# Exponentials of two pairs at once, rotating sum slots, and norms moved to GpSimd in a fused transformer, expert and state-space kernel

## The reference

```python
h = layernorm(x) * (1 + ca) + sa
x = x + ga * attention_block(h)       # linear attention with decay, then a silu layer
h = layernorm(x) * (1 + cb) + sb      # experts: 8 of 128 -> 512 -> 128
x = x + gb * sum_e weight_e * (gelu(h @ w1[e] + b1[e]) @ w2[e] + b2[e])   # top 2 of 8
h = layernorm(x) * ...                # state space, 256 channels, 16 states n
dA = exp(dt * A[:, n])                # 128 x 512 per channel half, state and chunk
H  = dA * H + (dt * xc) * B[n]        # a scan over the tokens
y  = sum_n H * C[n]; y = y * silu(z); x = x + ga * (y @ W_out)
h = layernorm(x) * ...                # real part of an inverse FFT of a weighted FFT
x = x + gb * (h @ w_fft + bias)
```

## Time and profile before

| | us |
|---|---|
| median of 3 runs (605.8 to 610.0) | 607.29 |
| the profiled execution | 606.43 |
| its span in the trace | 604.4 |
| TensorE busy | 482.4 (80%) |
| VectorE busy | 428.9 (71%) |
| ScalarE busy | 363.4 (60%) |
| GpSimd busy | 313.2 (52%) |

### The profile page before, as it was taken

How to read it: one execution, slowest core, us unless ns; L and a number is a source line. 1 busy time by engine, 2 the same in 40 slices (tenths; PEclk the granted TensorE clock), 3 DMA queues, 4 the chain that set the end, 5 groups by cost and what they waited for, 6 DMA issues and landing times.

```text
span 604.4 us, 6869 instructions
## 1 busy us (share of the span) xinstructions
PE 482.4 (80%) x2346; PEld 337.7 (56%) x2346; DVE 428.9 (71%) x723; ACT 363.4 (60%) x507; POOL 313.2 (52%) x220
## 2 busy tenths in 40 slices
PE   3869876769899999979869988789897497667573
PEld 3457544434588886757756677657586443233222
DVE  4766798964534334058997779997879985997961
ACT  0531442224664676689999999799988656634201
POOL 3224976866111011314686649767557946566541
PEclk9986999989999999999999989999989779897797
DMA  8700000000000000401866553765725703111000
GB/s 294 272 1 0 1 1 1 2 0 0 1 0 2 2 1 0 142 1 35 193 147 139 151 139 87 180 136 144 168 75 148 165 20 104 70 63 42 17 0 17
DMA packets 15010, 44.74 MB, mean 74 GB/s; under 512 B 2241, under 2 KB 7745, under 8 KB 12545
## 3 DMA queue, kind: packets, MB, share of 16 engines
q0 software_dynamic: 2448, 17.83, 14.5%
q1 hardware_dynamic: 11952, 25.57, 12.4%
q10 hardware_dynamic: 576, 0.92, 0.5%
HBM read 25.31 MB, written 1.18 MB: 44 GB/s over the span
## 4 chain that ended last, share of the span: by engine, by line
PE 24%; ACT 13%; DVE 12%; issue 6%; POOL 3%; DMA 3%; POOLq 0%; ACTq 0%; DVEq 0%
DVE Hs L761 6%; PE pO L1231 5%; DVE pCT L748 4%; ACT dA L985 3%; PE pY L1274 3%; PE pY L1317 3%; ACT gel L973 3%; PE pH L1219 2%; ACT L985 2%; ACT L973 2%; PE pH L1221 2%; PE pH L1220 2%; ACT ln_x L835 2%; PE pH L1274 2%; DMA Acc<-ZS 1%
## 5 line engine op out<-in xcount | busy, mean ns | idle before, releaser
L1231 PEld LDWEIGHTS pO<-w_e,gel 128*128 128x128 f32 x1024 | 124.8, 195 | 14.2 <-issue 8.8
L1231 PE MATMUL pO<-w_e,gel 128*128 128x128 f32 x1024 | 127.2, 279 | 1.4 <-DVE X L732 1.1
L761 DVE TENSOR_TENSOR_SCAN Hs<-dA,HL,pCT 128x512 f32<-128x512 f32 x96 | 117.7, 1268 | 8.1 <-POOL Zev L382 3.8
L382 POOL TENSOR_TENSOR ZS<-Hs,Crow 128x1024 f32<-128x1024 f32 x32 | 76.5, 2392 | 58.3 <-DVE Hs L761 58.3
L973 ACT ACTIVATE gel<-pH,b_e 128x512 f32<-128x512 f32 x128 | 85.9, 687 | 33.3 <-PE pH L1221 32.6
L985 ACT ACTIVATE dA<-dt,a_neg 128x512 f32<-128x512 f32 x128 | 81.9, 710 | 21.0 <-DVE Hs L761 20.7
L748 DVE TENSOR_TENSOR pCT<-u,pB 128x1024 f32<-128x1024 f32 x64 | 78.3, 1224 | 16.7 <-PE pB L1299 15.5
L1219 PE MATMUL pH<-h2h,w_e1h 128*128 128x512 f32 x128 | 57.8, 452 | 22.6 <-ACT gel L973 21.4
L382 POOL TENSOR_TENSOR Zev<-Hs,Crow 128x1024 f32<-128x1024 f32 x26 | 62.8, 2420 | 16.0 <-DVE Hs L761 15.2
L732 DVE SCALAR_TENSOR_TENSOR X<-pO,wts,X 128x128 f32<-128x128 f32 x128 | 35.9, 343 | 43.2 <-PE pO L1231 43.1
L438 POOL TENSOR_TENSOR ZA<-Qsb,S 128x1024 f32<-128x1024 f32 x16 | 38.0, 2374 | 33.6 <-DVE S L656 32.0
(11 more groups left out here) (225 smaller groups left out, 878.1 us busy)
## 6 DMA issues: line engine op xcount, KB each, us to landing
Crow<-c_rows SPq DMA_DIRECT2D x32, 512.0 KB, 4.0
Acc<-ZS POOLq DMA_DIRECT2D x10, 1024.0 KB, 8.5
Acc<-Zev POOLq DMA_DIRECT2D x7, 1024.0 KB, 7.7
w_e<-in_w_e SPq DMA_DIRECT2D x2, 2048.0 KB, 10.4
X<-in_x SPq DMA_DIRECT2D x4, 256.0 KB, 7.0
out<-h2T SPq DMA_DIRECT2D x4, 256.0 KB, 2.2
S<-in_w_mod ACTq DMA_DIRECT2D x2, 384.0 KB, 4.7
w_cx<-in_conv_row SPq DMA_DIRECT2D x1, 512.0 KB, 9.7
```

The source lines that it names most:

```text
L382: pool.tensor_tensor(Z, Hs[:, 2 * o:2 * o + 2, 0:w], Crow[:, 2 * (p % NCB) + o:2 * (p % NCB) + o + 1, 0:w].to_broadcast([P, ND, w]), ALU.m ...
L761: vec.tensor_tensor_scan(Hs[:, 2 * o + d, 0:w], dA[:, 4 * (p % 2) + 2 * o + d, 0:w], pU[:, d, 0:w], HL[:, d, n:n + 1] if c else 0.0, ALU.m ...
L1231: ins = mm(pO[:, j * P:(j + 1) * P], gel[:, n % NG, j * P:(j + 1) * P], w_e2[:, NK * (g % E) + k, :], start=(k == 0 and j == 0), stop=(k = ...
```

## The change

- `decays`: three groups of slots in dA; in odd pairs ScalarE makes the exponentials of pairs p+1 and p+2 in one go, in even pairs none.
- `pair`: up 0 and up 1 of expert g+1 are issued in pair p, between down 1 and the stages "B"; row_b of the next pair's first state moves ahead of down 1.
- The norm (`ln_apply`) goes from ScalarE to four GpSimd operations in `ln`; the two small ones that made its bias go. The cast of BCf to ST goes to GpSimd too.
- `ln_turn` of the next chunk moves from C of k = 4 to a new place "U" in k = 5: on TensorE after the first row_b and before up 2, on ScalarE between the second and third gelu.
- Zev, ZS and the two Acc become three rotating slots `Zt`: the sum of a chunk lies where the even pairs of the chunk before lay.

```diff
@@ later_stages
-                             (2, "end", "ln_stats", tail), (3, "apply", "ln_apply", tail), (3, "C", "ln_turn", tail, 2),
+                             (2, "end", "ln_stats", tail), (3, "C", "ln_turn", tail, 2),
-                    plan += [(4, "mid", "ln_stats", front), (4, "apply", "ln_apply", front), (4, "C", "ln_turn", front, 1),
+                    plan += [(4, "mid", "ln_stats", front), (5, "U", "ln_turn", front, 1),
...
@@ sums
+        def acc_of(c):
+            return Zt[:, 2 * (c % 2), :, 0:WIDTHS[c]]
+        def z_of(p):
+            c, k = divmod(p, NP)
+            if k == 0 and not alone(p):
+                return acc_of(c)
+            return Zt[:, 1 if k % 2 else 2 - 2 * (min(c, ALONE // NP) % 2), :, 0:WIDTHS[c]]
...
@@ gpsimd ln
-                pool.wait_ge(s["ln_xn"], L[0])
-                pool.tensor_scalar(ln_nm[:, 0:J], ln_mv[:, 0:J, 0], -1.0, None, ALU.mult)
                 link(pool.tensor_scalar(ln_ve[:, 0:J], ln_mv[:, 0:J, 1], EPS, None, ALU.add))
                 link(pool.tensor_tensor(ln_rs[:, 0:J], ln_ve[:, 0:J], mhalf[:, 0:J], ALU.pow))
-                pool.tensor_tensor(ln_nb[:, 0:J], ln_nm[:, 0:J], ln_rs[:, 0:J], ALU.mult).then_inc(s["ln_rstd"], 1)
+                pool.wait_ge(s["ln_tr"], L[0])
+                for j in range(J):
+                    ins = pool.tensor_scalar(ln_x[:, j, :], rows_of(X, c)[:, j, :], ln_mv[:, j, 0:1], ln_rs[:, j:j + 1],
+                                             ALU.subtract, ALU.mult)
+                ins.then_inc(s["ln_xn"], 1)
...
@@ gpsimd output
+                Z = z_of(p)[:, part, :]
                 if p >= ALONE + 2:
                     pool.wait_ge(s["mam_y"], totals(p - 2))
-                elif k == 0 and not alone(p):
-                    Z = Acc[:, c % 2, part, 0:w]
-                    if c >= 2:
-                        pool.wait_ge(s["mam_y2"], 2 * (c - 1))
...
+                elif p >= 2 and o == 0 and sums(p - 2):
+                    pool.wait_ge(mam_s[p % 2], 16 * sums(p - 2))
+                if k == 2 and c and p < ALONE + 2 and o == 0:
+                    pool.wait_ge(s["mam_y2"], 2 * c)
...
@@ gpsimd rows
+                link(pool.tensor_copy(st, bc))
...
@@ scalar decays
-                if p >= 2:
-                    act.wait_ge(s["mam_sc"], 4 * (p - 1))
+                if p >= 3:
+                    act.wait_ge(s["mam_sc"], 4 * (p - 2))
...
@@ scalar, the list
                 if 0 <= p + AHEAD < NL * E:
-                    hidden(p + AHEAD, range(NK))
-                if 0 <= p + 1 < NL * NP:
-                    decays(p + 1)
+                    hidden(p + AHEAD, (0, 1))
+                run(p, stages, "U")
+                if 0 <= p + AHEAD < NL * E:
+                    hidden(p + AHEAD, (2, 3))
+                for q in (p + 1, p + 2) if p % 2 else ():
+                    if 0 <= q < NL * NP:
+                        decays(q)
                 run(p, stages, "AB")
-                run(p, stages, ("apply",))
                 run(p, stages, "C")
...
@@ tensor pair
-                if moe:
-                    up(g, 0)
-                    up(g, 1)
+                if any(at == "U" for at, *_ in stages) and not moe:
+                    run(p, stages, "U")
                 if 0 <= p < NL * NP:
                     row_b(2 * p + 1)
+                if moe:
+                    run(p, stages, "U")
                 if moe:
                     up(g, 2)
                     up(g, 3)
...
                 if moe:
                     down(g, 0)
-                    down(g, 1)
                 if not early and 0 <= 2 * p + 2 < NL * NS:
                     row_b(2 * p + 2)
+                if moe:
+                    down(g, 1)
+                if g + 1 < NL * E:
+                    up(g + 1, 0)
+                    up(g + 1, 1)
                 run(p, stages, "B")
```

More of the change, by code:

```diff
@@ L157, in build @@
         rank = sb("rank", [P, NJ, E])
-        dA = sb("dA", [P, 2 * 2 * ND, TC])
+        dA = sb("dA", [P, 3 * 2 * ND, TC])
         Hs = sb("Hs", [P, 2 * ND, TC])
-        Zev = sb("Zev", [P, 2 * ND, TC])
-        ZS = sb("ZS", [P, 2 * ND, TC])
+        Zt = sb("Zt", [P, 3, 2 * ND, TC])
         Crow = sb("Crow", [P, 2 * NCB, TC])
@@ L210, in stage_bank @@
         def stage_bank(p, at):
-            return (2 if p < ALONE else 0) + int(at == "B")
+            return (2 if p < ALONE else 0) + int(at in ("B", "U"))
         def tail_bank(c):
@@ L283, in later_stages @@
             for stage in (("A", "total", NL * NP - 1), ("end", "gate", last), ("A", "project", last), ("end", "tail_x", last),
-                          ("end", "bias", last), ("mid", "ln_stats", last), ("apply", "ln_apply", last),
+                          ("end", "bias", last), ("mid", "ln_stats", last),
                           ("A", "ln_turn", last, 2), ("A", "fft", last)):
@@ L473, in rows @@
                 st, bc = ST[:, c % 2, 0:w], BCf[:, c % 2, 0:w]
-                pool.wait_ge(s["mam_st0"], c + 1)
-                pool.wait_ge(s["ln_rstd"], L[0])
+                pool.wait_ge(s["mam_bcs"], c + 1)
+                pool.wait_ge(s["ln_xn"], L[0])
                 for name, count in done.items():
@@ L497, in gate @@
                 for d in range(ND):
-                    pool.tensor_tensor(y2[:, d, 0:w], Acc[:, c % 2, d, 0:w], half_of(gz, c)[:, d, :],
+                    pool.tensor_tensor(y2[:, d, 0:w], acc_of(c)[:, d, :], half_of(gz, c)[:, d, :],
                                        ALU.mult).then_inc(s["mam_y2"], 1)
@@ L534, in ln_stats @@
                 Xc = rows_of(X, c)
-                vec.wait_ge(s["ln_rstd"], L[0])
+                vec.wait_ge(s["ln_xn"], L[0])
                 L[0] += 1
@@ L828, in _ @@
             nc.scalar.activation(silu_c[:, :], cols[:, COL["c0"]:COL["c0"] + 2], ACT.Silu).then_inc(s["silu_c_ready"], 1)
-            def ln_apply(c):
-                act.wait_ge(s["ln_rstd"], A[0] + 1)
-                act.wait_ge(s["ln_tr"], A[0])
-                for j in range(blocks(c)):
-                    ins = nc.scalar.activation(ln_x[:, j, :], rows_of(X, c)[:, j, :], ACT.Identity,
-                                               bias=ln_nb[:, j:j + 1], scale=ln_rs[:, j:j + 1])
-                ins.then_inc(s["ln_xn"], 1)
-                A[0] += 1
             def ln(dest, c, m, b, high=None):
@@ L950, in rows @@
                 nc.scalar.copy(BCf[:, c % 2, 0:w], PS[b][0:96, 0:w]).then_inc(s["mam_bcs"], 1)
-                act.wait_ge(s["mam_bcs"], c + 1)
-                nc.scalar.copy(ST[:, c % 2, 0:w], BCf[:, c % 2, 0:w]).then_inc(s["mam_st0"], 1)
             def dt_part(c, d, b):
@@ L996, in run @@
                         continue
-                    if stage == "ln_apply":
-                        ln_apply(c)
-                    elif stage in ("ln_turn", "route", "turn", "x_part", "rows", "dt_part", "z_part"):
+                    if stage in ("ln_turn", "route", "turn", "x_part", "rows", "dt_part", "z_part"):
                         {"ln_turn": turned, "route": route, "turn": turn, "x_part": x_part, "rows": rows, "dt_part": dt_part,
@@ L1312, in total @@
                 first = k == 0 or p == ALONE
-                Z = [Zev, ZS][p % 2]
+                Z = z_of(p)
                 for o in range(2):
@@ L1316, in total @@
                     for d in range(ND):
-                        ins = mm(pY[d][:, 0:w], ident[:, :], Z[:, 2 * o + d, 0:w], start=(first and o == 0),
+                        ins = mm(pY[d][:, 0:w], ident[:, :], Z[:, 2 * o + d, :], start=(first and o == 0),
                                  stop=(k == NP - 1 and o == 1))
@@ L1323, in total @@
                         for o in range(2):
-                            ins = mm(pY[d][:, 0:w], ident[:, :], Acc[:, c % 2, 2 * o + d, 0:w], start=False, stop=False)
+                            ins = mm(pY[d][:, 0:w], ident[:, :], acc_of(c)[:, 2 * o + d, :], start=False, stop=False)
                 ins.then_inc(s["mam_y"], 1)
```

22 lines of the change are left out of this document (6 added, 16 removed).

## The result

The changed kernel takes 651.65 us (median of 4 runs, 650.55 to 654.38) against 606.84 of the kernel before beside it: ratio 1.0748, 95% interval 1.071 to 1.0786. It is slower by 44.8 us, where 19.6 was forecast: the direction was right, the size was not, and 652 lies above the range of 603 to 638. The profiled execution took 650.55, its span 648.5.

The account below looks back on a forecast made before the run. It took a loop between TensorE and ScalarE, not one full engine, to bound the kernel. Mixed part +7.8, experts alone +4.2, norms and cast -1.8, clock +9.4 make +19.6: 626.0 for that execution, median 627; range 603 to 638 us.

Parts of the forecast that it names:

- The loop: Mixed part, odd pairs: eight exponentials stand before the next gelu, so up 2 to next up 2 takes 10.9 us.
- The other signs: Granted clock 0.50 three or more times a chunk; ScalarE some 10 us less busy per chunk; TensorE idle some 50 us.
- The clock: Half clock after eight TensorE standstills of 3.9 to 4.4 us, 1.3 each, less 1.0 for VectorE's slack: +9.4 us.
- the forecast's 7.8: Mixed part, clock apart: first chunk +4.7, next chunk +2.2, pair 15 to 16 +2.5, row_b -1.6; together +7.8 us.
- row_b (-1.6): From pair 16 to the start of pair 21, row_b comes 0.9 us or more sooner, ahead of down 1: -1.6 us.
- Pair 5 to 6: Loop 10.9, silu table 1.28, xc and BCf 1.2: 13.4 us from up 2 of k = 5 to that of 6.
- The ups ahead: Up 0 and up 1 issued early: experts alone +4.2 us together; pair k = 6 1.5 us more, 14.9 against 13.4.
- part of it returns as work done ahead: +2.4: First route: router's products come after up 1, up 2 moves from 165.24 to about 168.0; part returns, leaving +2.4 us.
- 0.3 each, nine times: -2.7: Experts alone: in pairs without a ScalarE stage the wait between up 1 and up 2 goes, -2.7 us.
- Norms and cast on GpSimd: GpSimd norm 0.4 each, 1.6 for four, mostly hidden by waits for scans; together -1.8 us, from +1.5 to -3.
- The clock holds: Rival: loop as worked out, but the clock stays full: +10.2 us, 617 us; chance 0.20.
- Relief arrives: Rival: exponentials do not hold TensorE, VectorE's work sets the chunk, 8 us less in two chunks: 589 us; chance 0.13.

Follow-up runs that it names:

- five filled standstills: Changed kernel with 14 unread TensorE products added at the end of pairs 1, 3, 9, 11 and 17 (pair 19 too): 637.83 us, ratio 1.0498.
- the block alone: Changed kernel keeping the eight exponentials in one go, with up 0 and up 1 in their own pair and norms and cast on ScalarE: 625.12 us, ratio 1.0321.
- the runs with fill: 14 unread TensorE products added in standstills: to the changed kernel, 637.83 us; to the block alone, 632.71 us, and in pairs 1, 3, 9, 17 only, 618.63 us.
- the one with none: Changed kernel with grouped exponentials, ups ahead and GpSimd norms and cast all undone; slots, third dA group, turn at U and row_b move stay: 602.86 us.

## Why the prediction was off, point by point

**The loop: right.** The step "on which the forecast rests" held. Odd mark to even mark was forecast at 10.9 and is 10.84 to 10.86 in the four plain odd pairs 1, 3, 9 and 17; the wait at the mark was to be 3.5 or more and is 3.55. The other signs came too: the clock at 0.50 four times in the chunk, ScalarE 12.5 less busy in it, 48.6 of idle before the ups. One chunk against the forecast:

| from k to k+1 | 7 to 0 | 0 to 1 | 1 to 2 | 2 to 3 | 3 to 4 | 4 to 5 | 5 to 6 | 6 to 7 |
|---|---|---|---|---|---|---|---|---|
| forecast, clock apart | 13.2 | 7.0 | 10.9 | 8.8 | 11.6 | 8.5 | 13.4 | 14.9 |
| measured (pairs 7 to 15) | 13.16 | 9.54 | 10.84 | 11.39 | 11.51 | 10.24 | 16.28 | 14.94 |

Four fit within 0.1. Three that follow a standstill are 1.7 to 2.6 too long: the clock. One, 5 to 6, is off by 2.9. The chunk was to take 88.3 without the clock and takes 97.9.

**The clock: mechanism right, size too small in this kernel.** "Half clock over 3.4 us costs 1.7; where part of it lies in the standstill less, 1.3 on average" took the length from the standstills of 1.9 us in the earlier trace rows. In the kernel after it is 6.8 us long behind seven of the eight, twice that. Even pairs cost 2.5 more than 7.0, and five filled standstills gave back 12.5. The term of 9.4 should have been some 20: eight times 2.5, an estimate from the 12.5 over five. With the block alone, where the half clock is mostly 3.4 long, the clock is some 11, near the 9.4; there it is the loop that was too small, 11 against the 6.4 that is left of the forecast's 7.8 without the ups (3.0) and row_b (-1.6). Nor does every standstill of 1.9 bring half clock: in the kernel before there is a third one, in front of mark 0 at 272.23, and the clock stays at 1.00 behind it. The Trainium skill (TensorE: Matmul & The Clock Gate, "HAM oscillation") gave the direction, and the runs with fill agree with it.

**Pair 5 to 6: the step that left out TensorE's order and clock.** "5: 10.9, silu table 1.28, xc and BCf 1.2, 13.4" followed ScalarE alone. Timeline of TensorE:

```profile
434.96 0.61 PE L1297 MATMUL pB<-ST,sel 96*128 96x512 bf16 x1 [2.75 <-DVE pCT L754]
435.36 4.78 PE L1272 MATMUL pY<-h3T,w_cx 128*128 128x512 f32 x8
...
443.16 1.02 PE L1278 MATMUL pY<-h3T,w_bc 128*96 128x512 f32 x2
...
446.85 0.50 PE L1212 MATMUL pH<-h2h,w_e1h 128*128 128x512 f32 x1 [0.67 <-ACT gel L965]
```

row_b stands in front of x_part and waits 2.75 for VectorE, which is behind; x_part then runs at half clock, 4.78 for 3.60. And w_bc stands behind the two ups ahead: BCf, the gelu table and the gelu come 1.5 later. I had priced just that for k = 6 ("the two ups ahead stand before both dt") and not for k = 5. Two runs separate the parts. With fill, row_b waits the same 2.75 but x_part takes 3.60, and the step is 14.92; with the ups in their own pair and x_part still at half clock it is 14.92 too. So some 1.4 is the clock and some 1.4 the ups, and next to nothing is left for VectorE's lateness by itself (the two runs change other pairs too). In the first chunk row_b waits 0.43, the clock is full, and the step takes 13.21.

**The ups ahead: the largest error.** Forecast 4.2 in the experts alone and 1.5 at k = 6 in two chunks, 7 in all; measured 21.9. The experts alone, mark by mark, kernel after against before, all counted from the reference row: the first mark was forecast 2.8 later and is 4.4 later (9.3 against 4.9). That it stands at 168.02, where 168.0 was forecast, is luck: this execution reached the reference row 1.6 sooner. The 1.6 is half clock, which is granted from about 161.3 to 164.7 under the two ups and the router; in the kernel with the ups alone the clock is 1.00 from 160 to 169 and the first mark is 2.8 later, as forecast, while the kernel with ups and block, the same code up to there, has 0.50 and is 4.4 later. Then "part of it returns as work done ahead: +2.4" failed. Nothing returns: at mark -11 the shift is 6.7 (18.5 against 11.8), for the wait of 2.77 brings half clock too (up 2 at 0.77 instead of 0.50), and the next pair takes 9.25 instead of 6.93. "0.3 each, nine times: -2.7" failed too: a plain pair takes 6.52 after and 6.72 before. The three triples with routing cost 0.8, 0.6 and 1.2, where +0.85 less the 0.3s had come to about nothing; 0.7 of the last is pair -3, forecast 0.8. Pair -2 to -1 cost 1.4 (forecast 1.5). Mark -1 came 10.7 later, forecast 4.2. In the mixed part k = 6 cost 1.4 each time, near the 1.5 of the forecast, but k = 5 and k = 7, at which the forecast had put nothing for the ups, cost 1.1 to 2.8 (kernel with the ups from pair 0 on). The run with the stage's products first shows that most of it, 16.2, is their order, not the two full banks.

**Norms and cast on GpSimd: wrong sign.** "I take 0.4, 1.6 for four, as on ScalarE": it is 0.79 each and 3.13 for four, just above the upper bound of 0.73. And "in the mixed part GpSimd waits for scans most of the time, which hides it" is half true. Counted in the run with norms alone against the one with none: -0.2 in the first chunk (mark -1 to 7), +1.6 from 7 to 16, and +3.4 behind it. Most of the last is two steps in the last chunk. GpSimd's multiplications for the states queue behind the norm of the chunk before, so the statistics come 12.6 after mark 19 instead of 11.0; then the norm itself, rows of GpSimd with norms there and of ScalarE without:

```profile
482.95 3.13 POOL L361 TENSOR_SCALAR ln_x<-X,ln_mv,ln_rs 128x128 f32<-128x128 f32 x4
```

```profile
476.65 1.65 ACT L840 ACTIVATE ln_x<-X,ln_nb,ln_rs 128x128 f32<-128x128 f32 x4 [4.00 <-POOL ln_nb L363]
```

From statistics to x_part it is 10.0 instead of 8.6. The cast took 0.60 against 0.62, nothing either way.

**Slots, third group, row_b: right but small.** Forecast 0 and -1.6, measured 3.1 below the kernel before, with the turn at U in it, which I had only as a product to be placed. Whether the turn or row_b gives the most of it is open.

**The sum, by parts.** Forecast: ups 7.2, norms -1.8, row_b -1.6, the block with its clock the rest of 19.6, 15.8. Measured: 21.9, 4.7, -3.1, 22.3, which is 45.8 against 44.8. So 14.7 of the missing 25 is the ups, 6.5 each the norms and the block.

**The rivals.** "The clock holds" is out: it fell behind each long standstill. "Relief arrives" is out: odd to even never fell below 10.8, far from the 8.8 from which it would decide. The GpSimd limit, at 640 and 0.06, had a true core: 0.79 is over its 0.73. But norms and cast account for 6.5 of the missing 25, and the time passed 640 by the ups. The block alone has the fewer table switches and is 3.2% slower than the kernel before, since the loop and not ScalarE's time bounded it; so the rule of the Trainium skill (ScalarE: Activation LUTs, "Table sets: the hidden batching unit") on grouping the calls of one set did not make this kernel faster.

**Open.** What makes the half clock 3.4 or 6.8 us long, and where the 3 us of the kernel with the slots only come from. Nor was the standstill behind pair -1 ever filled. Nor was the block tried in a place where TensorE has work of its own to cover it.

## What to carry to other kernels

When two engines pass work back and forth through two buffers, the time of a round is set by the longest stretch in which one of them gives the other nothing. Grouping what an engine does between its answers saves its time and lengthens that stretch; ask what covers the longest one, not what the sum is. And before work is moved ahead on an in-order queue, list every product that will now stand behind it and follow each to the engine that waits for it, for each kind of pair and not only for the plainest: here 1.5 us of "work done early" cost 16 by standing in front of a router and two small projections.

## What the runs showed that was not expected

- Half clock behind a standstill of 3.5 to 4.4 us lasted 3.4 or 6.8 us, both behind 3.7 in one execution of the kernel with the block alone. Adding 14 useless products of 3.5 us to a pair made the kernel faster, by 2% over six pairs.
- GpSimd takes 0.79 us for a 128x128 subtract and multiply with two values per partition (48 of them, 782 to 804 ns); ScalarE's four took 1.65 together, 0.48 each.
- The three faults add up to within 4 us in a kernel of four engines in a loop, where I had expected the block and the ups to make each other dearer.
